# Down projections of two feed-forwards with rounded and remainder weights in one 512-column product

## What is computed

```python
x = hidden_states
x = layernorm(x + attention(x))          # 16 heads, 128 + 64 rotary, 128 for values
x = layernorm(x + ffn0(x))               # silu(x W1') * (x W3'), transformed, then W2'
x = layernorm(x + mlstm_block(x))        # x1 = x + heads; x1 + (silu(h2 Wg) * (h2 Wu)) Wd
x = layernorm(x + ffn_int8(x))

def ffn0(x):
    hidden = fwht(silu(x @ W1.T) * (x @ W3.T))      # 1024 wide
    return hidden @ W2.T                             # back to 256
```

## Time and profile before

| | before |
|---|---|
| median of 3 runs | 673.78 us (673.56 to 674.79) |
| span of the profiled execution | 670.6 us |
| its own time | one of the three runs above; the result doesn't say which |
| mean granted TensorE clock | 0.995 of 2.4 GHz |
| TensorE busy | 658.1 us, 5297 products |
| VectorE busy | 438.3 us, 968 instructions |
| ScalarE busy | 411.3 us, 1085 instructions |
| GpSimd busy | 246.7 us, 279 instructions |

### The profile page before, as it was taken

One profiled execution on the slowest core, in us unless ns is written; L12 is line 12 of the kernel. 1 busy time (PEld: TensorE's weight loads), 2 busy tenths in 40 slices (PEclk: granted clock), 3 DMA queues, 4 the chain that ended last, 5 costly groups with the idle time before them and its releaser, 6 DMA issues. The chain is left out here.

```text
span 670.6 us, 15275 instructions
## 1 busy us (share of the span) xinstructions
PE 658.1 (98%) x5297; PEld 633.0 (94%) x5297; DVE 438.3 (65%) x968; ACT 411.3 (61%) x1085; POOL 246.7 (37%) x279
## 2 busy tenths in 40 slices
PE   8999999999999999999999999999999999999995
PEld 8999999999999999999999899999987799999995
DVE  6556557557666655765665576556569986556877
ACT  5556677666776666866577773334689864333553
POOL 3731972134353133632328555112451462222011
PEclk9999999999999999999999999999999899999999
DMA  7174654435534436534363404000166100000000
GB/s 254 37 219 160 193 172 140 133 101 174 168 127 113 127 108 185 161 128 126 97 183 124 111 1 151 32 0 2 48 208 243 65 1 1 1 1 0 1 33 31
DMA packets 38172, 69.74 MB, mean 104 GB/s; under 512 B 3440, under 2 KB 22640, under 8 KB 37872
## 3 DMA queue, kind: packets, MB, share of 16 engines
q1 hardware_dynamic: 37696, 68.38, 32.8%
q10 hardware_dynamic: 432, 0.79, 0.4%
HBM read 52.18 MB, written 16.97 MB: 103 GB/s over the span
## 5 line engine op out<-in xcount | busy, mean ns | idle before, releaser
L312 PE MATMUL PJ<-xTh,WBh 128*128 128x256 f32 x364 | 106.7, 293 | 0.3 <-POOL WBl L839 0.3
L314 PE MATMUL PJ<-xTh,WBl 128*128 128x256 f32 x364 | 103.0, 283 | 0.0
L313 PE MATMUL PJ<-xTl,WBh 128*128 128x256 f32 x364 | 102.8, 283 | 0.0
L824 POOL TENSOR_TENSOR stage<-stage 128x256 f32<-128x256 f32 x32 | 24.5, 766 | 165.0 <-DVE stage L691 165.0
L584 ACT ACTIVATE probs<-probs,rinv 128x256 f32<-128x256 f32 x128 | 58.4, 507 | 26.7 <-DVE rinv L707 26.7
L1202 PE MATMUL UG<-xTh,WBh 128*128 (+1 forms) x256 | 73.6, 288 | 0.3 <-PEq L54 0.3
L1205 PE MATMUL UG<-xTh,WBl 128*128 (+1 forms) x256 | 72.4, 283 | 0.0
L1203 PE MATMUL UG<-xTl,WBh 128*128 (+1 forms) x256 | 72.4, 283 | 0.0
L1274 ACT ACTIVATE ga<-UG 128x256 f32<-128x256 f32 x64 | 24.5, 383 | 75.1 <-PE UG L1205 75.1
L312 PEld LDWEIGHTS PJ<-xTh,WBh 128*128 128x128 f32 x364 | 69.6, 191 | 0.9 <-issue 0.5
L313 PEld LDWEIGHTS PJ<-xTl,WBh 128*128 128x128 f32 x364 | 69.6, 191 | 0.0
(11 more groups left out here) (320 smaller groups left out, 2385.9 us busy)
## 6 DMA issues: line engine op xcount, KB each, us to landing
K<-scr_k SPq DMA_DIRECT2D x60, 256.0 KB, 4.3
raw<-in_w_att SPq DMA_DIRECT2D x37, 256.0 KB, 4.7
Q<-scr_q SPq DMA_DIRECT2D x15, 512.0 KB, 7.5
stage<-scr_m SPq DMA_DIRECT2D x6, 768.0 KB, 5.9
scr_q<-rot_h SPq DMA_DIRECT2D x30, 128.0 KB
scr_q<-rot_l SPq DMA_DIRECT2D x30, 128.0 KB
scr_k<-rot_h SPq DMA_DIRECT2D x30, 128.0 KB
scr_k<-rot_l SPq DMA_DIRECT2D x30, 128.0 KB
```

The source lines that it names most:

```text
L312: pe.matmul(out, ah, bh, start=(i == 0), stop=False)
L313: pe.matmul(out, ah, bl, start=False, stop=False)
L314: last = pe.matmul(out, al, bh, start=False, stop=(i == n - 1))
L824: pool.tensor_tensor(y[:, 0:S], c[:, 0:S], sn[:, S:2 * S], ALU.subtract).then_inc(rope_sum, 1)
```

## The change

For kinds 0 and 1, fh times the rounded weights and fh times the remainder weights are one product with 512 columns of weights, which fills a whole bank of OUTS: columns 0 to 255 hold the sum with the rounded weights, 256 to 511 that with the remainders. fl times the rounded weights is added into columns 0 to 255, as before. VectorE adds columns 256 to 511 to the residual first, waits for that on a new semaphore (low_added), and adds columns 0 to 255. So that both kinds of weights can be read in one access, the remainder weights move into the second half of QKh, and fh into the first half of QKl. The second half of QKh still holds queries and keys of the attention's last step when GpSimd splits the down weights; so `split_down` waits for that head's scores.

```diff
--- before.py
+++ after.py
@@ -181,7 +181,7 @@
 
         def w_down(hi, i):
 
-            return (QKh if hi else QKl)[:, 0, i, :]
+            return QKh[:, 0 if hi else 1, i, :]
 
         def rope_bank(k, p):
 
@@ -903,6 +903,7 @@
                 pool.wait_ge(tail_hi, q + 1)
                 pool.tensor_copy(w_down(True, q), rope_f[:, q, :]).then_inc(had_split, 1)
                 pool.wait_ge(had_split, 2 * q + 1)
+                pool.wait_ge(scores_ready, 4 * (SLOTS - 1) + q + 1)
                 pool.tensor_tensor(w_down(False, q), rope_f[:, q, :], w_down(True, q).bitcast(F32),
                                    ALU.subtract).then_inc(had_split, 1)
 
@@ -955,7 +956,8 @@
         def halves(a):
 
             return [a[:, i, :, :].rearrange("p a (b d) -> p (a b) d", b=2) for i in range(2)]
-        (WDh, fh), (WDl, fl) = halves(QKh), halves(QKl)
+        (WDh, WDl), (fh, fl) = halves(QKh), halves(QKl)
+        WDpair = QKh[:, :, :, :].rearrange("p l a (b d) -> p l (a b) d", b=2)
         WLh, WLl = sb("WLh", [P, LP, PIECE], F32R), sb("WLl", [P, LP, PIECE], F32R)
 
         WI = sb("WI", [P, 12, PIECE], F32R)
@@ -1014,7 +1016,7 @@
 
         names = """wl_in wg_in small_in consts_set wg_hi wg_split wl_hi wl_split int8_in int8_done wm_hi wm_split
             ln_stats ln_aggr ln_var rstd_ready x_new ssq_ready ms_ready rms_ready xs_ready xs_copied
-            xt_ready xt_hi xt_split x_added scaled stored
+            xt_ready xt_hi xt_split x_added low_added scaled stored
             bgs_ready qk_ready qk_hi qk_split vog_ready v_taken og_ready gates_ready gates_tanh sp_ready
             chain_step m_ready nm_ready m_out masked_rows rows_ready gcol_ready enm_ready
             st_ready e_ready c_ready pv_ready vt_ready back_ready taken abs_ready nn_ready n2_ready n2_squared sq_ready msq_ready hv_ready
@@ -1219,27 +1221,30 @@
                     else:
                         pe.wait_ge(s_["x_added"], N_ADD[AFTER[kind]] + c)
                 for t in range(TT):
-                    rows = slice(t * P, (t + 1) * P)
-                    out = OUTS[:, t, 0:D]
-                    pe.matmul(out, fh[:, ht, rows], w_down(kind, ht), start=(ht == 0), stop=False)
-                    last = pe.matmul(out, fl[:, ht, rows], w_down(kind, ht), start=False,
-                                     stop=(kind == 2 and ht == FT - 1))
-                    if kind != 2:
-                        last = pe.matmul(out, fh[:, ht, rows], w_down(kind, ht, False), start=False,
-                                         stop=(ht == FT - 1))
+                    down_hi(t, ht)
+                    last = down_lo(t, ht, ht == FT - 1)
                 last.then_inc(q["down"], 1)
 
+            def down_hi(t, ht):
+
+                rows = slice(t * P, (t + 1) * P)
+                if kind == 2:
+                    return pe.matmul(OUTS[:, t, 0:D], fh[:, ht, rows], w_down(kind, ht), start=(ht == 0), stop=False)
+                return pe.matmul(OUTS[:, t, :].rearrange("p (l d) -> p l d", l=2), fh[:, ht, rows], WDpair[:, :, ht, :],
+                                 start=(ht == 0), stop=False)
+
+            def down_lo(t, ht, stop):
+
+                return pe.matmul(OUTS[:, t, 0:D], fl[:, ht, t * P:(t + 1) * P], w_down(kind, ht), start=False, stop=stop)
+
             def last_down(ht):
 
-                at = [slice(t * P, (t + 1) * P) for t in range(TT)]
                 pe.wait_ge(q["f_hi"], FT * (B - 1) + ht + 1)
                 for t in range(TT):
-                    pe.matmul(OUTS[:, t, 0:D], fh[:, ht, at[t]], w_down(kind, ht), start=False, stop=False)
-                    if kind != 2:
-                        pe.matmul(OUTS[:, t, 0:D], fh[:, ht, at[t]], w_down(kind, ht, False), start=False, stop=False)
+                    down_hi(t, ht)
                 pe.wait_ge(q["f_lo"], FT * (B - 1) + ht + 1)
                 for t in range(TT):
-                    last = pe.matmul(OUTS[:, t, 0:D], fl[:, ht, at[t]], w_down(kind, ht), start=False, stop=(ht == FT - 1))
+                    last = down_lo(t, ht, ht == FT - 1)
                 last.then_inc(q["down"], 1)
 
             def step(c, ht, first):
@@ -1301,6 +1306,10 @@
             src = OUTS[:, :, 0:D]
             if kind == 1:
                 dve.wait_ge(s_["x1_mid"], c + 1)
+            if kind != 2:
+                part = N_ADD[AFTER[kind]] + c + 1
+                dve.tensor_tensor(res_v[:, c, :, :], OUTS[:, :, D:2 * D], res_v[:, c, :, :], ALU.add).then_inc(s_["low_added"], 1)
+                dve.wait_ge(s_["low_added"], part)
             if kind == 2:
 
                 dve.wait_ge(s_["x_added"], N_ADD[4] + c)
```

## The result

The change made the kernel slower by a little: the ratio to the kernel before is 1.0022, with a 95% interval of 1.0014 to 1.0030, that is +1.5 us (0.9 to 2.0). The medians are 674.75 us with the change and 672.69 us before, over 19 runs each in turn; they are 2.1 us apart, just above that interval. The three runs of before that were shown ahead of the prediction (median 673.78) lay high.

A forecast was written before the change was run, and what follows sets the result against it. TensorE was taken as the bound, together with the chain from residual add to next transposition. 2.4 us saved, 1.9 lost at three transpositions and a tail, gave -0.5 us: 673.3 us from 673.78, 8-in-10 range 671.7 to 674.9.

The forecast's parts named there:

- The chain behind the second add: From residual add through statistics and scaling to TensorE's next transposition: 0.71 us later per batch, less TensorE's earlier savings.
- main case: Whole kernel: 2.4 us saved, 1.9 lost at three transpositions and a tail, giving -0.5 us, 673.3 us; chance 0.62.
- rival 2: Down products of the first two feed-forwards: only 2.5 to 7 ns saved per place, +0.6 to +1.1 us; chance 0.16.
- I take 19 ns: Each of 128 down-product places: 512 plus 256 columns replace three 256-column products, saving 19 ns, bounds 7 and 22.
- the term of 2.4 us: TensorE time saved over the first two feed-forwards: 128 places at 19 ns each.
- the recorded steps: Transposition-by-transposition sums of TensorE's saving against the 0.71 us add, over the first two feed-forwards: -0.5 us.
- The reserve of batch 1 of kind 1: Second feed-forward, batch 1: copy ready at 573.28, transposition at 574.28; just covered, no wait, shift -0.58 us.
- The second add: VectorE adds the low columns after waiting on its own first add: 0.71 us more per batch, 0.79 upper bound.
- The last batch of kind 0: First feed-forward, batch 3: no reserve, wait about 1.2 us instead of 0.32, later saving lost; shift -0.16 us.
- Batches 2 and 3 of kind 1: Second feed-forward: waits of some 0.55 and 0.35 us before the transpositions, shifts -0.32 and -0.27 us.
- What was covered: No hole before a batch's first down product or in the other batches; GpSimd's wait on scores costs nothing.
- Rival 3: First feed-forward's batch 3 scaling and second's copies, beside GpSimd: chain 1.44 us late, +3.8 us, 677.6 us; chance 0.08.

The follow-up runs named there:

- joint_no_second_add: The changed kernel without the second add, so the remainder weights' half is left out of the result: ratio 0.9988 to the kernel before, -0.8 us.
- joint_contiguous: The changed kernel with the joint product reading 512 neighbouring columns of the rounded weights instead of two pieces of 256: ratio 1.0014 to the kernel before.
- after_early_wl: The changed kernel with GpSimd's split of the fifth piece of WL moved ahead of the first feed-forward's loop: ratio 1.0006 to the kernel before.
- joint_three_edits: The changed kernel with both joint products first, WL's fifth piece split early, and second feed-forward transpositions one tile later: ratio 0.9959 to before, median 670.36 us.

## Why the prediction was wrong

The forecast was -0.5 us, the result is +1.5 (0.9 to 2.0). The chain behind the second add was the right mechanism, but the term it was weighed against was too large, and one wait was read from one of its two conditions. That the time itself, 674.75 us, lies within the range is no merit of the main case: the range reached so far up for rival 2. The prediction called 0.2% the limit of "same", and 0.22% (0.14 to 0.30) stands on that limit.

- **The step that failed** is "I take 19 ns, because the changed order always has a 256-column product right behind a 512-column one". A place saved 6 ns (0.77 us over 128 places, joint_no_second_add), so the term of 2.4 us was 0.8. The row it was read from has eight products of 512 columns in a row and one of 256 behind them; a sequence that alternates had no row. The rows of the attention gave 7 ns, the lower bound that I had, and were the better guide. Put into the recorded steps, 6 ns and 0.71 us give +0.8 us in place of -0.5. This was the size of rival 2, which had 0.16; its reason, the two pieces of weights, did not hold (joint_contiguous). What makes the joint product slower in this order stays open.
- **The reserve of batch 1 of kind 1** was read from the copy of xs alone ("copy ready at 573.28, transposition at 574.28 ... Just covered"). The transposition also needs the bank TB, which VectorE still reads for the transposition before. That read (L1143) ended at 574.07 in the kernel before, so the reserve was 0.07 us and not 0.86. Here is the row of before:

```profile
573.21 0.86 DVE L1143 SCALAR_TENSOR_TENSOR xTl<-TB,cols,xTh 128x256 fp32r<-128x256 f32 x2
```

  It explains the wait of 0.56 us where none was forecast. With this read in the recorded steps, beside the 6 ns, they give +1.4 us; the two stages measured +1.23. So it is the smaller part of the miss.
- **The second add** was priced right: 0.72 us from start to start where 0.71 was said.
- **The last batch of kind 0** was described right: a wait of 1.09 us was measured where about 1.2 was said, and the saving behind it was lost. Kind 0 came out 0.45 us longer; 0.71 less 23 tiles at 12 ns is 0.43.
- **Batches 2 and 3 of kind 1** waited 0.27 and 0.26 us, where 0.55 and 0.35 were said: TensorE itself was less early, by the smaller saving. In batch 2 the chain was also shorter by almost 0.2 us than the steps say, for which no run gives a reason.
- **What was covered** was covered: no hole before a batch's first down product, none in batches 1 and 2 of kind 0, none at GpSimd's wait on scores.
- **The rule** of the Trainium skill (TensorE: Matmul & The Clock Gate, "Back-to-back issue gap"), 2.5 ns saved at a place, was nearer to the measured 6 ns than my 19. The section gives it for a product by itself and not for a stream of products with weight loads, and each of its pitches was off here: 256 columns took 120 ns here, not 109, and 512 took 233 to 241, not 216.
- **Rival 3**, the growth of the chain by more than one add, did not happen; the sign turned without it. A slip without effect: from 467.43 to 468.03 six down products start, and not five.

## What to carry to other kernels

If you price a new instruction order, take it from rows that have the same neighbours, and where there are none, keep the row of the mixed case and not the best one. For every wait that stands near the critical engine, list all that it waits for (the data and the buffer), and take the smallest reserve: an instruction added to a chain costs its length wherever that reserve is smaller. A change that trades work of the bounding engine for work on a chain behind it can be turned around by moving what waits: here three small edits made a loss of 0.2% a gain of 0.4%.

## What the runs showed of the hardware

- The pitch of fp32r products depended on their order here. Behind a joint product of 512 columns that followed one of 256, the next started after 0.24 us; in a row of 512-column products it was 0.2275. Putting two of each side by side made the two stages 0.57 us shorter. Whether the moving weights came in one piece or two, or from another tensor, made no difference.
- Two scalings of 256 columns on VectorE took 2.04 us beside GpSimd's split, and 0.62 when the split was moved away: 1.4 us. The second of them alone took 1.44 us, from 467.41 to 468.85, beside GpSimd's subtraction of 1.27, from 467.43 to 468.70. The Trainium skill's rule that VectorE and GpSimd lock a shared port pair ("SBUF — State Buffer", "Who interferes with whom") agrees with this; the runs show the overlap and its cost, not the port.
- The granted clock fell in the middle stage in some profiles. In that of the fastest kernel, by stretch (length, busy PE, PEld, DVE, ACT, POOL, clock, DMA share, GB/s):

```profile
510.00:520.00 10.00, 9.71 (x107) 7.39 (x105) 9.00 (x21) 9.52 (x29) 3.95 (x4) 0.92 0.53 195
520.00:530.00 10.00, 10.00 (x83) 7.60 (x84) 7.71 (x18) 6.75 (x19) 2.06 (x4) 0.74 0.18 73
```

  A clock of 0.74 between the levels is time at 1.2 and at 2.4 GHz mixed. TensorE waits for short times in the mLSTM heads in every profile, with and without a fall, so these profiles don't show what brings it about. This stage took 68.61 us there and 68.54 in after_early_wl, 67.0 to 67.1 in the five profiles where one stretch of 10 us was granted 0.83, and 66.4 to 66.6 where the clock stayed at 1.00. That is 2 us, more than the whole change is worth. Both profiles with the deep fall are of kernels with the split of WL moved; the kernel before seems to have it too: two of its 29 runs beside joint_three_edits show a clock of 0.990 over the whole run, and 675.8 and 676.0 us, where the median was 672.99. Whether the moved split makes it more frequent, the runs don't tell.
